# A four-block graph layer on one core: the steps of the first hop and of the last stage written out on all engines, without loops

## The reference

```python
def _spmm(edge_src, edge_dst, edge_weight, feats, n_nodes):
    msgs = edge_weight[:, None] * feats[edge_src]
    return jax.ops.segment_sum(msgs, edge_dst, num_segments=n_nodes)
...
feats = [x]
cur = x
for _ in range(n_blocks - 1):
    cur = _spmm(edge_src, edge_dst, edge_weight, cur, n_nodes)
    feats.append(cur)
concat = jnp.concatenate(feats, axis=1)
return concat @ shared_weight + output_bias
...
x = _layernorm(x + _L0_gnn_ref(...), axis=-1)
```

## Time and profile before

| | us |
|---|---|
| median of 3 runs | 1682.57 |
| lowest, highest | 1680.76, 1683.73 |
| the profiled execution | 1681.41 |
| its span, first to last instruction | 1679.5 |

### The profile page before, as it was taken

One profiled execution on the slowest core, in us unless ns is written; L12 is line 12 of the kernel. 1 busy time (PEld: TensorE's weight loads), 2 busy tenths in 40 slices (PEclk: granted clock), 3 DMA queues, 4 the chain that ended last, 5 costly groups with the idle time before them and its releaser, 6 DMA issues.

```text
span 1679.5 us, 36209 instructions
## 1 busy us (share of the span) xinstructions
PE 1567.3 (93%) x8468; PEld 1335.7 (80%) x8468; DVE 1169.2 (70%) x4883; ACT 1145.9 (68%) x3038; POOL 1065.6 (63%) x1044
## 2 busy tenths in 40 slices
PE   6799999999999999978978999969999999999993
PEld 5688888888888888757757888758888888888882
DVE  6867777777777778986644545437777777777773
ACT  3687777777777766656754655537777777777774
POOL 2277777777777731556774555547777777777764
PEclk9999999999999999999989999989999999999996
DMA  7499999999999986658986777767888888888852
GB/s 254 164 354 337 338 335 338 338 335 336 329 332 338 341 273 232 215 173 276 365 277 180 210 211 202 182 184 260 274 265 276 278 278 280 283 275 271 269 197 91
DMA packets 217722, 451.09 MB, mean 269 GB/s; under 512 B 30444, under 2 KB 125993, under 8 KB 217622
## 3 DMA queue, kind: packets, MB, share of 16 engines
q1 hardware_dynamic: 167730, 343.20, 58.5%
q0 software_dynamic: 49456, 106.58, 22.3%
q10 hardware_dynamic: 436, 0.20, 0.0%
HBM read 232.78 MB, written 225.74 MB: 273 GB/s over the span
## 4 chain that ended last, share of the span: by engine, by line
PE 77%; DVE 10%; issue 5%; DMA 3%; POOL 2%; ACT 1%; DVEq 0%; POOLq 0%; SPq 0%; ACTq 0%
PE ps_y L1218 32%; PE ps_u L1284 9%; PE ps_xT L1209 8%; PE ps_sum L1251 6%; PE ps_sum L1423 5%; PE ps_u L1423 5%; PE ps_u L1278 3%; DVE y_ring L1492 3%; PE ps_list L1384 2%; PE ps_u L1384 2%; DVE stats L1498 2%; PE ps_u L1417 1%; PE ps_sum L1417 1%; DMA c_rows<-sums,scatter_idx 1%; PE ps_u L1377 1%
## 5 line engine op out<-in xcount | busy, mean ns | idle before, releaser
L1218 PE MATMUL ps_y<-w_sb,xT 128*128 128x256 f32 x3128 | 808.5, 385 | 16.0 <-DVE y_ring L1492 16.0
L1218 PEld LDWEIGHTS ps_y<-w_sb,xT 128*128 128x128 f32 x3128 | 566.3, 193 | 78.2 <-issue 16.3
L1492 DVE TENSOR_TENSOR y_ring<-ps_y,bias 128x512 f32<-128x512 f32 x391 | 270.0, 691 | 251.4 <-PE ps_y L1218 250.5
L943 ACT ACTIVATE o_ring<-y_ring,shift,rstd 128x256 f32<-128x256 f32 (+1 forms) x782 | 421.7, 590 | 0.1
L930 ACT COPY xT<-ps_xT 128x512 f32<-128x512 f32 x391 | 227.3, 581 | 202.3 <-PE ps_xT L1209 194.5
L1498 DVE BATCH_NORM_STATS2 stats<-y_ring 128x6 f32<-128x256 f32 (+1 forms) x782 | 291.3, 415 | 4.8
L707 POOL DMA_INDIRECT tails_found<-tail_keys,table_idx x200 | 201.0, 1005 | 124.0 <-issue 69.9
L1209 PE MATMUL ps_xT<-ident,x_ring 128*128 128x128 f32 x1564 | 240.6, 277 | 23.7 <-ACT xT L930 14.7
L707 POOL DMA_INDIRECT rows_in<-in_x,gather_idx x200 | 202.4, 1012 | 81.7 <-issue 68.7
L711 POOL DMA_INDIRECT out_rows<-u_out,tailo_idx x197 | 197.4, 1002 | 85.8 <-issue 39.9
L707 POOL DMA_INDIRECT rows_in<-in_x,tailx_idx x197 | 201.8, 1024 | 77.7 <-issue 47.0
(11 more groups left out here) (231 smaller groups left out, 2100.2 us busy)
## 6 DMA issues: line engine op xcount, KB each, us to landing
x_ring<-in_x SPq DMA_DIRECT2D x195, 512.0 KB, 5.9
out_rows<-o_ring SPq DMA_DIRECT2D x195, 512.0 KB, 4.0
c_rows<-zeros SPq DMA_DIRECT2D x50, 512.0 KB
c_rows<-sums SPq DMA_DIRECT2D x50, 512.0 KB
u_rows<-u_out SPq DMA_DIRECT2D x50, 512.0 KB, 4.0
keys_bc<-keys_out SPq DMA_DIRECT2D x64, 256.0 KB, 5.1
keys_bc<-u_rows SPq DMA_DIRECT2D x25, 512.0 KB, 5.5
tails_found<-u_rows SPq DMA_DIRECT2D x12, 512.0 KB
```

Source lines behind the costliest of these rows:

```text
L943: last = act.activation(o_ring[slot][0:rows, r * D:(r + 1) * D], y_ring[k][0:rows, r * D:(r + 1) * D], ACT.Identity, bias=shift[k][0:rows, ...
L1218: last = pe.matmul(ps_y[bank][0:rows, r * D:(r + 1) * D], xT[bank][:, q * P:q * P + rows], w_sb[:, c, :], start=c == 0, stop=c == KC - 1)
L1492: dve.tensor_tensor(y_ring[k][0:rows, half * 2 * D:(half + 1) * 2 * D], ps_y[half][0:rows, :], bias2[0:rows, :], ALU.add).then_inc(y_copie ...
```

## The change

The constants of the loops go, both helpers run over all steps in Python, and DVE's first hop calls the helper like the others. Every step of the two stages is then in the program by itself, with constants in place of registers. What is computed, the tiling, the buffers, the waits and the order of work on each engine are as before.

```diff
-    A_FIRST, A_TURN = 3, 3
-    A_TURNS = (A_STEPS - A_FIRST) // A_TURN
-    A_LAST = A_FIRST + A_TURN * A_TURNS
-    D_TURNS = D_STEPS // 2 - 2
-    assert PAIR * A_TURN == RING and A_FIRST % 3 == A_TURN % 3 == 0 and D_STEPS % 2 == 0
...
-        def each_a_step(eng, run):
-
-            for a in range(A_FIRST):
+        def each_a_step(run):
+
+            for a in range(A_STEPS):
                 run(a, a_step(a), a % 3)
-            with eng.Fori(0, A_TURNS) as h:
-                for i in range(A_TURN):
-                    run(A_TURN * h + A_FIRST + i, a_step(A_FIRST + i, h), i)
-            for a in range(A_LAST, A_STEPS):
-                run(a, a_step(a), a % 3)
-
-        def each_d_step(eng, run):
-
-            for d in range(2):
-                run(d, d_step(d), d, 0)
-            with eng.Fori(1, D_TURNS + 1) as h:
-                for d in range(2):
-                    run(2 * h + d, d_step(d, h), d, h)
-            for d in range(D_STEPS - 2, D_STEPS):
+
+        def each_d_step(run):
+
+            for d in range(D_STEPS):
                 run(d, d_step(d), d % 2, d // 2)
...
-            each_a_step(sp, step_a)
+            each_a_step(step_a)
...
-            for a in range(A_STEPS):
-                step_a(a, a_step(a), a % 3)
+            each_a_step(step_a)
```

More of the change, by code:

```diff
@@ L651, in _ @@
                 load_u(g, g)
-            each_d_step(sp, step_d)
+            each_d_step(step_d)
             for u in range(UNITS - STEP, UNITS):
@@ L743, in _ @@
             limit(SLOTS)
-            each_a_step(pool, step_a)
+            each_a_step(step_a)
             def list_group(g, k):
@@ L887, in _ @@
                 gather_d(k, k, 0, 0)
-            each_d_step(pool, step_d)
+            each_d_step(step_d)
             for k in range(G):
@@ L1054, in step_a @@
                         count_tiles(a + 1, q)
-            each_a_step(act, step_a)
+            each_a_step(step_a)
             for l in range(LIST_ALL):
@@ L1176, in last_units @@
                     normalise(u, 0, UNITS % RING, UNITS // RING, 0, TAIL_P)
-            each_d_step(act, lambda d, dense, par, turn: step_d(d, lambda q: dense_slot(dense, q)))
+            each_d_step(lambda d, dense, par, turn: step_d(d, lambda q: dense_slot(dense, q)))
             step_d(D_STEPS, last_units)
@@ L1314, in _ @@
             pe.wait_ge(tables_ready, 1)
-            each_a_step(pe, step_a)
+            each_a_step(step_a)
             for l in range(LIST_ALL):
@@ L1444, in last_pairs @@
                         multiply_part(2 * UNITS, 0, m, TAIL_P)
-            each_d_step(pe, lambda d, dense, par, turn: step_d(d, lambda q: dense_slot(dense, q)))
+            each_d_step(lambda d, dense, par, turn: step_d(d, lambda q: dense_slot(dense, q)))
             step_d(D_STEPS, last_pairs)
@@ L2060, in last_measures @@
                     unit_shift(UNITS, 0, TAIL_P, TAIL_RPP)
-            each_d_step(dve, lambda d, dense, par, turn: step_d(d, par, turn, lambda q: dense_copy(dense, q),
+            each_d_step(lambda d, dense, par, turn: step_d(d, par, turn, lambda q: dense_copy(dense, q),
                                                                lambda q: dense_measure(dense, q)))
```

## The result

| | before, us | after, us |
|---|---|---|
| median | 1682.88 | 1684.88 |
| lowest, highest of 20 runs each | 1680.56, 1685.49 | 1681.14, 1687.27 |
| the profiled execution's span | 1679.5 | 1685.4 |

The ratio is 1.0015, with a 95% interval of 1.0008 to 1.0021. The change costs 2.0 us, which is within the 0.2% that the text took as no change. The profiled execution of after is one of its slowest (1687.09 us), so the 5.9 us between the two spans are more than the change is worth. Two things separate its effect from the rest: what comes back once a step, and where the difference arises. Both kernels run the same 8468 matmuls in the same order, so the start of each can be compared with its twin's.

A forecast was written before the change was run, and what follows sets the result against it. PE, 93% busy, was taken as the bound. 1681.41 + 0 (back edges) - 0.2 (registers) + 0.5 (fetch) = 1681.7 us for the profiled execution; +0.3 on the 1682.57 median gives 1682.9 us, range 1680.0 to 1686.5.

The forecast's parts named there:

- Back edges: Loop iterations removed in the first hop and last stage; claimed worth 0, bounds 0 to PE's 2.04 us of idle time.
- Register work: Registers computed before waits and addresses in both loops become constants; part says 0, bounds 0 to -1.2 us; sum takes -0.2.
- Fetching the code: More instruction packets for both written-out stages; claimed +0.5 us, bounds 0 and +15 us.
- the hesitation of the earlier trace: VectorE's 0.57 us gap at 417.35 us in the first hop, PE idle 0.43 us behind it; possibly a code fetch.
- Outside the loops: Stops around the last stage, in code not looped or whose loop stays; claimed 0, each may move some tenths.
- The two stops of the earlier trace: PE's waits around the last stage, 11.2 us for first gathered rows, 9.1 us for the late tile's; expected within a microsecond.
- The marks: Signs expected in the changed profile: PE idle, step periods, q8 and q14 packets, fewer instructions, the two border stops.
- late code: Slower rival: PE's code packets in both stages come late, 0.43 us each, all 33 giving 1696.8 us; chance 0.07.
- Control costs more than PE shows: Faster rival: dropped control work gains more, 1680.5 us inside the loops, 1676.8 us if border stops shrink; chance 0.04.

The follow-up runs named there:

- a_pe: The kernel before with the first hop written out on PE alone, other engines as before; 0.9985 of before on a slower chip.
- before_fast: The kernel before, loops kept, with VectorE's u_out copy of a step's first slot moved ahead of its index staging; 0.9975 of before on a slower chip.
- after_swap: The changed kernel with PE's two waits ahead of its turn of the sums in the other order; 1911.01 us on a slower chip.
- after_swap2: Repeat of after_swap, the changed kernel with PE's two waits exchanged; 1905.58 us, 0.975 of before on a slower chip.

## Why the prediction was right, and where it wasn't

- **The forecast** was 1682.9 us in a range of 1680.0 to 1686.5, with 0.89 for no change; 1684.88 us lies in it, 0.15% above before. The reading that carried it, that the kernel already held both forms and that their periods agree, holds to 0.01 us in the last stage and missed by 0.06 us in the first hop. The 21.92 us that I took for a written step there is no test of the written form: it runs from 113.95 to 135.87 us and so holds the looped turn of the sums at 133.87 us, with its load 52 ns behind u_out. After, the same period is 21.92 us too, with the load at 115 ns, so what makes it long is something else. The two turns in written steps, at 111.94 and 593.11 us, lie outside the periods that I compared.
- **Back edges, 0.** Borne out: no gap of PE came or went at one, and over the last stage the twins' starts drift apart by no more than 0.01 us.
- **Register work, -0.2 us with bounds of 0 to -1.2.** The part itself says 0 and the sum takes -0.2; by either, this is the step that failed. I took the register instructions for work that could only cost, put the wait for u_out aside as belonging to VectorE's unchanged code, and left the rest of PE's idle time, 1.2 us, to the control. But all of the 2.04 us was this wait. The register instruction carried one of two waits, and taking it away moved the other, the one that ends last, to a slower place: +62 ns * 21 = +1.3 us. The bound should have reached above zero: where an edit changes what instructions stand between two waits, the latency of the later one can change on the waiting engine.
- **Fetching the code, +0.5 us.** The packets came as forecast, 72 and 109 against 68 and 103, and about evenly. The last stage took its share, 52 of them, without a gap. In the first hop, gaps of 0.51 us at 421.64 and 0.46 us at 575.38 stand at the steps where before had 0.43 at 418.30 and 0.38 at 571.58. They aren't new, so I see no cost of the fetch, and the hesitation of the earlier trace rows was no measure of it. Nor was it the only one, as the prediction has it: the stop at 571.58 us stood in the same trace.
- **Outside the loops, 0.** The two stops of the earlier trace rows are 10.9 and 9.0 us:

```profile
PE ps_u L1401 <- DMA rows_in<-in_x,tailx_idx: 10.9, 1, 10.9
PE ps_xT L1440 <- DMA rows_in<-in_x,latex_idx: 9.0, 1, 9.0
```

- **The marks.** Right: the last stage without idle time, the mean periods, the packets, the stops. Wrong: 3.93 us of PE idle in the first hop, where I had said 1 to 3.
- **Accounting.** Of the +2.0 us, 1.2 to 1.3 are the moved wait. That it moved, that its latency doubled and that exchanging the waits undoes the latency is shown, and that the first hop became 1.20 us longer is read from one trace of each kernel. That this is the wait's price is worked out, since no run on the first chip had it alone. The other 0.7 or 0.8 us are open: the interval reaches from 1.3 to 3.5 us, and a share of runs at the lower clock between 40 and 60 us would do it. The median lies 2.0 us above the middle of the forecast. Its place in the range is in part luck: the upper side was made wide for late code and the scatter of the runs, and what was shown to come is neither.
- **The rivals.** Late code didn't come. "Control costs more than PE shows" was wrong on the chip I predicted for. On two others the change does gain 2%, more than that rival's best case, by a mechanism that isn't shown. I had argued against it from 2.04 us of PE's idle time, and in the kernels traced there with most of their loops, a_pe and before_fast, PE is idle for 286 us.

## What to carry to other kernels

Where an engine waits for two things ahead of one instruction, look at which of the two its own instruction carries, and order the code so that it is the one that ends last; a loop's register computation may be doing this for you unseen. Before costing an edit of control at nothing because the bound engine is never idle, ask whether it is also never idle on another chip. A written-out step next to a looped one in the same trace is good evidence, but compare the places where the bound engine waits, instruction by instruction, and make sure that the period which you call written holds no looped one of them: here the 62 ns of 21 steps were to be seen at those places and not in the periods. And where two kernels run the same instructions in the same order, compare the start of each with its twin's; that tells in which stage a difference arises.

## What the runs showed of the hardware

- A wait carried by a weight load lets it start 52 or 53 ns behind the end of VectorE's instruction; one that stands in an instruction of PE's sequencer ahead of the load, 114 to 116 ns. This held in every kernel on all three chips, but for single places (the spreads are 51 to 54 and 114 to 118 ns, with a handful of others between 69 and 162).
- Loop bodies of these sizes were held once loaded (20 steps with 6 packets). PE's body of three steps is one of about three packets of 16 KB: writing out 18 more of its steps in a_pe took q8 from 35 to 54. Straight-line code of both stages, 81 more packets, was fetched beside DMA engines 98% and 82% busy without a new stop of PE.
- The granted clock between 40 and 60 us differs between executions of one program (after_swap 0.91, after_swap2 0.74), and 2.6 us went with such a difference between the traces of before and after.
- Chips differ. The same program took 1683 us on one and 1952 to 1956 us on two others, with equal median durations of single matmuls but 238 us of PE's idle time in gaps over 0.3 us in the changed kernel where the first chip had 85. On those chips SyncE's register moves at times took up to 716 ns where SyncE has its loops (a_pe); on the first, 29 to 42 ns.
